# Cross-attention with a routed feed-forward layer on one core: V's projection at every fifth score tile instead of every third, and 24 instead of 27 key tiles of exponentials on VectorE

## What is computed

```python
x = x + _L0_xattn_ref(_layernorm(x), ctx_768, ...)     # x 1024 x 128, ctx_768 6404 x 96
x = x + _L0_ffn_ref(_layernorm(x), ...)

# _L0_xattn_ref: 16 heads of size 8, scale 8 ** -0.5
q = query @ Wq + bq;  k = key_value @ Wk + bk;  v = key_value @ Wv + bv
attn = softmax(clip(einsum('bhqd,bhkd->bhqk', q, k) * scale, -CLAMP, CLAMP))
out = einsum('bhqk,bhkd->bqhd', attn, v).reshape(B, Nq, Cq) @ Wo + bo

# _L0_ffn_ref: a main two-layer network with gelu, and the 2 best of 8 experts
# chosen by softmax(mean(x) @ w_gate + b_gate)
```

## Time and profile before

| | us |
|---|---|
| median of three runs | 785.53 |
| lowest and highest | 785.46, 788.52 |
| the profiled execution's own time | 788.86 |
| its span, first to last instruction | 786.9 |
| TensorE busy | 733.3 |
| ScalarE busy | 718.1 |
| VectorE busy | 564.5 |

### The profile page before, as it was taken

The page is one execution under the profiler, slowest core; times in us unless marked ns, Lnnn a source line. Parts: engine busy times, 40 slices in busy tenths (PEclk is TensorE's granted clock), DMA queues, the critical chain, the costliest instruction groups (busy, mean ns, idle before and its releaser), DMA issues.

```text
span 786.9 us, 13292 instructions
## 1 busy us (share of the span) xinstructions
PE 733.3 (93%) x5412; PEld 219.2 (28%) x5412; DVE 564.5 (72%) x789; ACT 718.1 (91%) x574; POOL 28.8 (4%) x50
## 2 busy tenths in 40 slices
PE   6999989999999999999999999999999999999898
PEld 3534322222222222222222222222222222222457
DVE  6944178798878978797788897897789773139320
ACT  4868999999999999999999999999999999999351
POOL 5240000000000000000000000000000000000000
PEclk9979999999999999999999999999999999999999
DMA  5678100011110000111100000111100000000010
GB/s 163 203 179 254 31 1 1 21 47 35 34 35 1 2 0 2 34 37 49 51 2 1 1 1 18 45 41 35 34 1 1 1 1 2 1 1 1 2 55 27
DMA packets 18043, 28.53 MB, mean 36 GB/s; under 512 B 5286, under 2 KB 8732, under 8 KB 17980
## 3 DMA queue, kind: packets, MB, share of 16 engines
q1 hardware_dynamic: 12730, 23.71, 10.1%
q0 software_dynamic: 4032, 3.30, 1.8%
q10 hardware_dynamic: 1218, 0.64, 0.3%
HBM read 19.50 MB, written 8.13 MB: 35 GB/s over the span
## 4 chain that ended last, share of the span: by engine, by line
PE 58%; ACT 19%; issue 16%; DVE 3%; DMA 2%; POOLq 0%; SPq 0%; POOL 0%; ACTq 0%
PE po L1232 31%; PE ps L1147 17%; ACT region_ctx L533 14%; ACT probs_own L533 5%; PE ps L1327 2%; PE po L1048 2%; DMA k_dram<-kparts 1%; PE po L1337 1%; PE po L1218 1%; PE ps L1037 1%; DVE pT L632 1%; PE po L1147 1%; DMA xres<-in_x 1%; PE po L1124 1%; DMA region_ctx<-in_w1e 0%
## 5 line engine op out<-in xcount | busy, mean ns | idle before, releaser
L533 ACT ACTIVATE region_ctx<-ps 128x1536 f32<-128x1536 f32 x375 | 528.5, 1512 | 12.7 <-PE ps L1147 12.4
L1232 PE MATMUL po<-region_ctx,v 128*9 128x512 f32 x2238 | 392.0, 598 | 0.5 <-ACT region_ctx L533 0.5
L1147 PE MATMUL ps<-qst,region_k 32*128 32x512 f32 x1492 | 251.1, 493 | 36.6 <-ACT region_ctx L533 26.3
L1147 PEld LDWEIGHTS ps<-qst,region_k 32*128 32x128 f32 x1492 | 96.5, 182 | 408.3 <-ACT region_ctx L533 289.9
L1232 PE MATMUL po<-probs_own,v 128*9 128x512 f32 x746 | 192.9, 598 | 0.5 <-ACT region_ctx L533 0.5
L533 ACT ACTIVATE probs_own<-ps 128x1536 f32<-128x1536 f32 x125 | 189.1, 1513 | 3.3 <-PE ps L1147 2.9
L840 DVE TENSOR_SCALAR region_kT<-po 128x512 f32<-128x512 f32 x108 | 74.1, 686 | 86.1 <-PE po L1147 86.1
L843 DVE SCALAR_TENSOR_TENSOR region_kT<-region_kT,po 128x512 f32<-128x512 f32 x108 | 73.5, 680 | 0.3
L881 DVE SCALAR_TENSOR_TENSOR dres<-region_kT,dres 128x1024 f32<-128x1024 f32 x54 | 66.1, 1225 | 1.7
L878 DVE SCALAR_TENSOR_TENSOR dres<-region_kT,dres 128x1024 f32<-128x1024 f32 x54 | 65.8, 1218 | 0.2
L870 DVE SCALAR_TENSOR_TENSOR dres<-region_kT 128x1024 f32<-128x1024 f32 x54 | 65.8, 1218 | 0.0
(11 more groups left out here) (216 smaller groups left out, 352.4 us busy)
## 6 DMA issues: line engine op xcount, KB each, us to landing
region_k<-k_dram SPq DMA_DIRECT2D x40, 320.0 KB, 3.3
k_dram<-kparts SPq DMA_DIRECT2D x18, 320.0 KB, 4.2
qst<-q_dram POOLq DMA_DIRECT2D x12, 128.0 KB, 9.9
region_ctx<-in_ctx SPq DMA_DIRECT2D x2, 624.0 KB, 9.4
q_dram<-dres POOLq DMA_DIRECT2D x2, 512.0 KB, 3.1
k_dram<-kparts SPq DMA_DIRECT2D x2, 322.0 KB, 3.6
region_ctx<-in_ctx SPq DMA_DIRECT2D x1, 576.0 KB, 7.8
xres<-in_x SPq DMA_DIRECT2D x1, 512.0 KB, 4.4
```

The lines of the kernel that those rows point to most:

```text
L533: act.activation(probs_of(t), ps[t % NSB][:, :], ACT.Exp, scale=ESCALE).then_inc(exp_ready, 1)
L1147: return mm(dst, kst[r, kt * P:(kt + 1) * P], qst[r, g, queries], start=True, stop=True)
L1232: last = mm(dst[QUAD * j:QUAD * j + V9, :], w, src, start=first, stop=last_one, skip_group_check=True)
```

## The change

Three tables of numbers are changed. V's chunks 2 to 12 stand at tiles 4, 9, 14, ..., 54 instead of 2, 5, 8, ..., 32. The small jobs of the first pass move by one to three tiles. `D_PLAN` has 24 D tiles instead of 27, the first score at tile 59 instead of 37; the first pass has none now and the last one instead of three. Three D tiles fewer are twelve chunks more for ScalarE, so there are 504 score tiles instead of 500.

```diff
--- before.py
+++ after.py
@@ -55,8 +55,8 @@
 
 
 NPRE = 14
-V_AT = {c: 3 * c - 4 for c in range(2, VCH)}
-BOUND_TILES, GSUM_TILE, ROWS_TILE = (3, 7), 10, 12
+V_AT = {c: 5 * c - 6 for c in range(2, VCH)}
+BOUND_TILES, GSUM_TILE, ROWS_TILE = (6, 8), 11, 13
 CB = HID // P
 MIX_BANK = 5
 NORM_GAP = 2
@@ -85,33 +85,30 @@
 
 
 D_PLAN = [
-    (0, 49, (37, 39, 42, 44), (0, 2, 3, 1), 56),
-    (1, 49, (48, 51, 57, 60), (1, 2, 0, 3), 75),
-    (1, 48, (64, 71, 73, 78), (0, 1, 3, 2), 91),
-    (1, 47, (81, 84, 87, 91), (3, 0, 1, 2), 103),
-    (1, 46, (94, 97, 103, 107), (2, 3, 1, 0), 119),
-    (2, 29, (110, 113, 116, 123), (2, 3, 0, 1), 138),
-    (2, 39, (126, 133, 135, 140), (1, 2, 0, 3), 154),
-    (2, 49, (143, 146, 149, 154), (0, 1, 2, 3), 166),
-    (3, 49, (157, 160, 163, 170), (2, 3, 0, 1), 197),
-    (3, 48, (173, 176, 179, 186), (2, 3, 0, 1), 201),
-    (3, 47, (189, 196, 198, 203), (1, 2, 0, 3), 217),
-    (3, 46, (206, 209, 212, 217), (0, 1, 2, 3), 229),
-    (3, 45, (220, 223, 226, 233), (2, 3, 0, 1), 245),
-    (4, 29, (236, 239, 242, 249), (2, 3, 0, 1), 264),
-    (4, 49, (256, 258, 261, 267), (1, 3, 0, 2), 280),
-    (4, 48, (270, 273, 276, 280), (3, 0, 1, 2), 292),
-    (4, 47, (283, 286, 292, 296), (2, 3, 1, 0), 308),
-    (5, 49, (299, 302, 305, 311), (2, 3, 0, 1), 327),
-    (5, 48, (318, 320, 323, 329), (2, 0, 1, 3), 343),
-    (5, 47, (332, 335, 338, 343), (0, 1, 2, 3), 355),
-    (6, 19, (346, 349, 352, 359), (2, 3, 0, 1), 382),
-    (6, 29, (362, 365, 368, 374), (2, 3, 0, 1), 390),
-    (6, 49, (381, 383, 386, 392), (2, 0, 1, 3), 406),
-    (6, 48, (395, 398, 401, 406), (0, 1, 2, 3), 418),
-    (7, 49, (409, 412, 415, 422), (2, 3, 0, 1), 453),
-    (7, 48, (425, 428, 431, 477), (2, 3, 0, 1), 489),
-    (7, 47, (479, 481, 485, 488), (3, 1, 0, 2), 499),
+    (1, 49, (59, 61, 64, 73), (2, 0, 1, 3), 83),
+    (1, 48, (75, 77, 82, 84), (1, 3, 2, 0), 99),
+    (1, 47, (88, 91, 95, 101), (0, 1, 2, 3), 115),
+    (2, 19, (104, 107, 110, 117), (0, 1, 2, 3), 138),
+    (2, 34, (120, 123, 126, 136), (0, 1, 2, 3), 146),
+    (2, 49, (138, 140, 145, 147), (1, 3, 2, 0), 162),
+    (2, 48, (151, 154, 158, 164), (0, 1, 2, 3), 178),
+    (3, 49, (167, 170, 173, 180), (0, 1, 2, 3), 197),
+    (3, 48, (183, 186, 190, 199), (0, 1, 2, 3), 209),
+    (3, 47, (201, 203, 208, 210), (1, 3, 2, 0), 225),
+    (3, 46, (214, 217, 221, 227), (0, 1, 2, 3), 241),
+    (4, 24, (230, 233, 236, 243), (0, 1, 2, 3), 260),
+    (4, 34, (246, 249, 258, 263), (0, 1, 3, 2), 276),
+    (4, 49, (266, 269, 272, 279), (3, 0, 1, 2), 292),
+    (4, 48, (282, 285, 288, 295), (3, 0, 1, 2), 308),
+    (5, 49, (298, 301, 304, 311), (3, 0, 1, 2), 327),
+    (5, 48, (321, 323, 326, 331), (3, 1, 2, 0), 343),
+    (5, 47, (334, 337, 340, 347), (2, 3, 0, 1), 359),
+    (5, 46, (350, 353, 356, 363), (2, 3, 0, 1), 375),
+    (6, 34, (366, 369, 372, 382), (2, 3, 0, 1), 394),
+    (6, 49, (384, 386, 390, 393), (3, 1, 0, 2), 406),
+    (6, 48, (397, 400, 403, 406), (2, 3, 0, 1), 418),
+    (6, 47, (410, 413, 419, 422), (1, 2, 0, 3), 434),
+    (7, 49, (425, 428, 434, 474), (2, 3, 1, 0), 481),
 ]
 DKT = [[kt for p, kt, *_ in D_PLAN if p == q] for q in range(NP)]
 STEPS = [(p, kt) for p in range(NP) for kt in range(FULL + 1) if kt not in DKT[p]]
```

## The result

Ten executions of the changed kernel took 791.05 us in the median (789.54 to 793.93), ten of the kernel before 786.98 (785.44 to 792.35). The ratio is 1.0055 with a 95% interval of 1.0036 to 1.0074: about half a per cent slower, where I had forecast 787.5 and "the same".

A forecast was written before the change was run, and what follows sets the result against it. ScalarE's exponentials, 1.33 us a tile, were taken as the bound nearly everywhere, TensorE's work in wrong rounds adding to it. 5.32 - 2.7 + 1.2 - 1.7 + 0.9 - 1.0 = +2.0 on 785.53 gave 787.5 us, range 784.2 to 790.5.

The forecast's parts named there:

- Until tile 17: -2.7: First stage: two V chunks fewer save 2.18 us, a 0.89 wait for VectorE goes, 0.37 of new waits come.
- third rival: Up to tile 17: the early gain of 2.7 us is taken back, giving 790.2 us; chance 0.14.
- Tiles 17 to 64: +1.2: Eight V chunks instead of six: six in full rounds at 0.82 us, two in free rounds at 0.2.
- first rival: V's spaced chunks are nearly hidden, only 0.25 us each left; tile 64 comes 3.3 us earlier, 784.2 us; chance 0.16.
- From tile 64 on: -1.7: Excess over 1.33 us per tile, 14.24 before, falls by 1.7 in four parts, between -3.5 and +1.
- first_main wait: Last first_main, near tile 477: the next score job waits until VectorE has taken the fourth first_main, +0.9 us (none to 1.5).
- (d): Pass ends with two values steps in one round cost about 1.4 us, otherwise 0.7; five of seven instead of three: +1.3.
- (a): Six places where a D tile's last score shares a round with another's values step disappear: 6 x 0.3 = -1.8 us.
- (b): Two D steps fewer from tile 64 on: -0.3 us.
- (c): Two crowded places, around D steps 119 and 197/201, cost 0.66 and 0.54 us; none stands so now: -0.9.
- The end: -1.0: Behind the last exponential two values steps stand in line instead of three: -1.0 us.
- second rival: At three pass starts with close scores TensorE waits for VectorE, ScalarE loses about 2 us each time: 793.5 us; chance 0.08.

The follow-up runs named there:

- D steps moved later: Kernel before, with the values steps of six D tiles one free round later (91 to 95, 154 to 158 and so on): 786.3 us, ratio 0.9991.
- the last score job later: Changed kernel, with the last score job at tile 478 instead of 474 and its values step at 489 instead of 481: 790.83 us, ratio 1.0039.
- V in free rounds with gaps: Changed kernel, with V's chunks 2 to 12 only in free rounds, 4 to 52, leaving free rounds 20 and 36 empty: 789.64 us, ratio 1.0034.
- scores moved earlier: Kernel before, with the last scores of six D tiles one or two rounds earlier (91 to 90, 154 to 152 and so on): 788.07 us, ratio 1.0.
- the kernel before with chunks in free rounds: Kernel before with its 27-tile plan, V's chunks 2 to 12 moved so that eight of eleven stand in free rounds, the last at 36: 790.3 us.
- both repairs: Changed kernel, with V's chunks in free rounds 4 to 52, 20 and 36 empty, and the last score job at 478, its values step at 489: 787.46 us.
- the plan alone: Changed kernel's 24-tile plan, but V's chunks and the small jobs where the kernel before had them: 793.35 us, ratio 1.0065.
- both versions with V in free rounds: Changed kernel, V's chunks at every free round, 4 to 44 (790.42 us), or at 4 to 52 with free rounds 20 and 36 empty (789.64 us).

## Why the prediction was wrong

The predicted difference was +2.0 us, the measured one +4.9 to +5.1 at equal clock or stretch and +4.1 between the medians. Besides, 787.5 was put on a median of 785.53 from three runs. The ten executions of before beside the changed kernel have 786.98, which is 1.45 of the 3.55 us by which the time was missed, and the 73 whose clock is on record have 787.4. The profiled execution that I made the sum against had an unusually long half-clock stretch; its 788.86 + 2.0 = 790.9 meets the 791.13 of the profiled execution after only because that one's stretch was shorter.

**Four more tiles, +5.32: right.** They run at 1.33 us each, and no engine covers any of it. The Trainium skill (ScalarE: Activation LUTs, What ACT_TABLE_LOAD costs) would have 1.37; the traces on both sides have 1.33.

**"Until tile 17: -2.7": failed, -1.15 measured.** Two chunks fewer are 2.18 us of work less. The wait of 0.89 which I subtracted is read rightly, and none of the three profiles with the changed order has it; but with the old order it comes and goes with the landing of a K store, and it is 0 in the profile compared here. And TensorE's new waits are 1.04 instead of the 0.37 I had walked out. TensorE of the changed kernel, again:

```profile
54.62 0.50 PE L1144 MATMUL ps<-qst,region_k 32*128 32x512 f32 x3
55.55 1.13 PE L1045 MATMUL po<-wv_sb,region_ctxT 97*128 97x128 f32 x8 [0.43 <-DVE gcol L721]
...
63.61 0.50 PE L1144 MATMUL ps<-qst,region_k 32*128 32x512 f32 x3 [0.61 <-ACT region_ctx L530]
```

I missed the first: the chunk of tile 9 comes in the round behind the second bound job (tile 8), and has only one score tile ahead of it, in which VectorE doesn't finish with that job's result. The second is the wait for exponentials, larger than I thought. -2.18 + 0.43 + 0.61 = -1.14, the measured figure. That it agrees to 0.01 us is luck: the two further profiles of this stretch are 0.14 apart. By either pair my third rival, that the early gain is taken back, came true at least by half.

**"Tiles 17 to 64: +1.2": the mechanism right, the size off, +0.43.** Chunks in full rounds cost 0.5 to 0.9 us whatever their distance, and the exponential that is missed shows three tiles later. ScalarE, first profile, behind the chunks of tiles 29, 34 and 39:

```profile
86.36 1.45 ACT L530 ACTIVATE probs_own<-ps 128x1536 f32<-128x1536 f32 x1 [0.49 <-PE ps L1144]
87.76 4.21 ACT L530 ACTIVATE region_ctx<-ps 128x1536 f32<-128x1536 f32 x3
...
93.80 4.20 ACT L530 ACTIVATE region_ctx<-ps 128x1536 f32<-128x1536 f32 x3 [0.49 <-PE ps L1144]
...
101.25 2.79 ACT L530 ACTIVATE region_ctx<-ps 128x1536 f32<-128x1536 f32 x2 [0.56 <-PE ps L1144]
```

The stage's excess is 4.55: 0.74 on average for the six in full rounds (I took 0.82) and nothing for the two in free ones (I took 0.2), with 0.09 left over from the stage ahead. So my first rival, spaced chunks nearly hidden, is false. The Trainium skill (TensorE: Matmul & The Clock Gate, Back-to-back issue gap) would have 0.65 us for a chunk; it takes 1.09 at full clock in every trace here.

**"From tile 64 on: -1.7": the step that failed.** With the first_main wait (0.95, predicted 0.9) taken off the measured 6.00 - 5.32 = +0.68, it is -0.3. Part (d), the pass ends, was right: counted from two tiles ahead of a pass's last tile to six behind it, the seven ends cost 6.0 us before and 7.3 now, +1.3 as predicted (+1.0 to +1.5 with the bounds set a tile or two elsewhere). The dearest is that of the sixth pass, two gaps within four tiles:

```profile
556.24 1.45 ACT L530 ACTIVATE probs_own<-ps 128x1536 f32<-128x1536 f32 x1 [0.68 <-PE ps L1144]
557.65 2.86 ACT L530 ACTIVATE region_ctx<-ps 128x1536 f32<-128x1536 f32 x2
561.44 1.46 ACT L530 ACTIVATE region_ctx<-ps 128x1536 f32<-128x1536 f32 x1 [0.92 <-PE ps L1144]
```

So (a), (b) and (c) together gave -1.6 us where I had put -3.0. This is 1.4 of the 3.1 us by which the sum is off; the stage up to tile 17 is 1.5.

In (c) the step "none stands so now" is false. The crowded places around D steps 119 and 197/201 are gone; their tiles 118 to 126 and 196 to 208 had 0.65 and 0.54 us of excess. But three others have come: tiles 260 to 268 have 0.63, 342 to 350 have 0.67 and 359 to 366 have 0.47 (means of the two profiles). ScalarE at the second of them, tiles 340, 344, 348 and 352, first profile:

```profile
506.30 1.62 ACT L530 ACTIVATE probs_own<-ps 128x1536 f32<-128x1536 f32 x1
...
511.88 1.45 ACT L530 ACTIVATE probs_own<-ps 128x1536 f32<-128x1536 f32 x1
...
517.52 1.45 ACT L530 ACTIVATE probs_own<-ps 128x1536 f32<-128x1536 f32 x1
...
522.93 1.47 ACT L530 ACTIVATE probs_own<-ps 128x1536 f32<-128x1536 f32 x1
```

Twelve tiles take 16.63 us there instead of 15.96. Crowded places cost 1.8 us now and 1.2 before, with three D steps in either: +0.6, where I had -0.9.

In (a), "6 x 0.3 = -1.8" is too much. I had compared a round with a D step and a lone score with a D step alone at 0.07 to 0.17. The six places cost 0.39 each, and 18 D steps of the changed kernel that stand by themselves 0.16 on average, which would make 1.4. The run with D steps moved later saved 1.0 us at the places and lost 0.6 again at the D steps behind, 0.4 in all; in the changed plan most D steps stand 16 tiles apart and not 8, so how much of the 0.6 is lost there is not shown. (b) had no run of its own either. So the sum of the three parts is measured and the falsehood of (c) is seen in the starts, but the split between (a), (b) and what is left stays open.

**"The end: -1.0": right, then lost again.** Behind the last exponential stand two values steps. The chain that ended last, first profile, where the earlier trace rows has three:

```profile
730.73 1.46 ACT region_ctx L530
732.23 1.04 PE po L1229 x8
733.28 1.02 PE po L1215 x8
```

From the last exponential's start to the end of these it is 3.57 us, 4.54 before. But the last store, the result's, lands later. SyncE's wait for it before the end, in the kernel before and the changed one, both profiled again:

```profile
SPq L193 <- DMA result<-xn: 1.4, 1, 1.4
```

```profile
SPq L190 <- DMA result<-xn: 2.4, 1, 2.4
```

It is 2.3, 2.4 and 2.6 us in the three profiles of the changed kernel and of the one with the last score job later, and 1.4 in all nine others. So it seems to belong to the program, though no instruction near it differs, and it is 1.0 of the 3.3 us by which the span of "V in free rounds with gaps" is shorter at equal clock. (0.4 us of these come back outside the span, see below, which leaves the 2.9.) Its cause stays open. That the part behind the last exponential is still 0.4 shorter comes from the load of the experts' weights in its chain, 3.77 us against 4.17.

**The second rival**, VectorE as what TensorE waits for, did not decide the time, but two runs show it waiting just behind: scores can't be moved forward in the one with scores moved earlier, and a V chunk one tile ahead of the D scores held TensorE up by 1.82 us in the kernel before with chunks in free rounds.

## What to carry to other kernels

When every round of the critical engine's feeder is nearly full, a piece of work costs what is left of it after the next empty slot, so count slots and leave one empty between two pieces; in these kernels the distance in tiles did not matter otherwise. A dear round with two extra pieces is not all saving when they are taken apart: ask what each costs where it would go instead, and what stands next to it there. When a plan is said to have no crowded place, look for the new ones. Before a sum is made against one profiled execution, look at where its clock was granted, and profile the kernel twice; a wait that is there in one execution may be absent in the next, above all one that ends with a transfer.

## What the hardware showed that I had not expected

Apart from the last 0.6 us of some spans, TensorE was granted half clock for one stretch in every profile but one, with another length from execution to execution of the same program: 10.2 and 6.8 us in two of the kernel before, 3.4 and 6.8 us in two of the changed one, none with both repairs. It begins near 40 us (in one profile at 103.5). 0.001 of mean clock is 0.79 us of a span of 788, or 1.58 us at half clock, so the fitted 0.66 us per 0.001 is 0.42 us lost for each us at half clock; this is most of the scatter of 784 to 791 us between executions of the kernel before.

The time outside the span was 1.9 to 2.0 us for the kernel before and the changed one, and 2.3 in the median for four others whose tables alone differ (the plan alone, both versions with V in free rounds of the changed kernel, and both repairs). I don't know why.
